# Routing two of four token batches of a mixture inside the memory attention ahead of it

## The reference, cut to what matters

```
x1: n = rmsnorm(layernorm(x)) * w;  K rows: n and the memory's keys;  attention over both
    g = sigmoid(layernorm(x) @ Wg + bg); x += the attended value mixed with layernorm(x) by g
f1: xn = layernorm(x)
    p = softmax(xn @ gate_w + gate_b)           # 8 experts
    two experts of largest p, shares p / (p_1 + p_2 + 1e-9)
    y = mlp_shared(xn) + sum over the two of share * mlp_expert(xn)   # 128 -> 512 gelu -> 128
    x = x + xn + y
```

## Time and profile before

| | |
|---|---|
| median of three runs | 2326.48 us |
| the profiled execution, its own time | 2327.09 us |
| its span, first to last instruction | 2325.2 us |
| busy in the span: PE, DVE, ACT, POOL | 76%, 57%, 47%, 32% |
| memory attention, first VectorE to last VectorE instruction | 884.0 to 990.4 us |
| first mixture, its routing and shared expert | 991.3 to 1113.1 us |
| first mixture, its 39 routed blocks, gather and add | 1113.1 to 1284.1 us |

### The profile page before, as it was taken

The page is one execution under the profiler, slowest core; times in us unless marked ns, Lnnn a source line. Parts: engine busy times, 40 slices in busy tenths (PEclk is TensorE's granted clock), DMA queues, the critical chain, the costliest instruction groups (busy, mean ns, idle before and its releaser), DMA issues. The chain is left out here.

```text
span 2325.2 us, 39403 instructions
## 1 busy us (share of the span) xinstructions
PE 1763.3 (76%) x14513; PEld 1214.8 (52%) x14513; DVE 1321.2 (57%) x3525; ACT 1103.7 (47%) x2265; POOL 746.2 (32%) x713
## 2 busy tenths in 40 slices
PE   3887561799996996859996685887788868751994
PEld 1555441545553664646896452655555535451774
DVE  2888578512235774563343465885379979851223
ACT  3676440333345776723442243773357657610431
POOL 1223200271364321057354002331223232156453
PEclk9888795699997998968998686999879969955997
DMA  4111272036624101112576001000000010011224
GB/s 154 83 82 83 90 241 69 15 104 168 181 54 171 78 2 47 28 40 99 172 234 206 10 1 33 24 20 10 3 1 2 2 37 29 11 45 66 69 77 139
DMA packets 143730, 173.19 MB, mean 74 GB/s; under 512 B 20913, under 2 KB 118897, under 8 KB 142609
## 3 DMA queue, kind: packets, MB, share of 16 engines
q1 hardware_dynamic: 123956, 129.09, 18.0%
q0 software_dynamic: 13248, 28.21, 3.6%
q10 hardware_dynamic: 6336, 13.37, 1.5%
HBM read 126.84 MB, written 79.05 MB: 89 GB/s over the span
## 5 line engine op out<-in xcount | busy, mean ns | idle before, releaser
L2773 POOL DMA_INDIRECT f_back<-f_ys,f_row x158 | 151.7, 960 | 175.8 <-DVE f_ys L2934 146.6
L2766 POOL DMA_INDIRECT f_slots<-f_pay,f_slot x128 | 124.6, 973 | 66.0 <-issue 38.1
L874 PE MATMUL a_AV<-a_vx,a_pT 128*64 128x18 f32 (+1 forms) x3072 | 115.1, 224 | 33.0 <-DVE a_two L544 15.3
L874 PEld LDWEIGHTS a_AV<-a_vx,a_pT 128*64 128x64 f32 x3072 | 105.9, 146 | 62.2 <-issue 28.6
L736 ACT ACTIVATE a_e<-a_e 128x512 f32<-128x512 f32 x192 | 110.2, 622 | 59.0 <-DVE a_e L566 58.9
L861 PE MATMUL a_TP<-ident,a_e 128*128 128x128 f32 x768 | 108.0, 285 | 19.9 <-ACT a_e L736 19.3
L741 ACT COPY a_pT<-a_TP 128x512 f32<-128x512 f32 x192 | 103.5, 588 | 39.5 <-PE a_TP L861 39.4
L861 PEld LDWEIGHTS a_TP<-ident,a_e 128*128 128x128 f32 x768 | 89.2, 146 | 57.5 <-ACT a_e L736 48.3
L566 DVE TENSOR_TENSOR a_e<-a_S,a_mx 128x1024 f32<-128x1024 f32 x96 | 117.3, 1222 | 2.9
L850 PE MATMUL a_S<-a_kbd,a_qT 64*64 64x512 f32 x768 | 114.2, 670 | 1.0 <-issue 0.6
L3000 ACT ACTIVATE f_h<-f_H,f_wt 128x256 f32<-128x256 f32 x156 | 67.1, 474 | 81.2 <-PE f_H L3096 81.2
(11 more groups left out here) (481 smaller groups left out, 4573.3 us busy)
## 6 DMA issues: line engine op xcount, KB each, us to landing
f_wt<-in_f_ew SPq DMA_DIRECT2D x39, 584.0 KB
f_slots<-in_blank SPq DMA_DIRECT2D x1, 18576.0 KB
f_wt<-in_f_leaf SPq DMA_DIRECT2D x94, 98.0 KB, 2.0
f_pay<-f_back SPq DMA_DIRECT2D x8, 1024.0 KB, 8.1
f_xs<-f_slots SPq DMA_DIRECT2D x47, 144.0 KB
memory_x_k<-w_stage ACTq DMA_DIRECT2D x24, 256.0 KB, 3.1
f_slots<-in_blank SPq DMA_DIRECT2D x1, 5760.0 KB
f_xs<-leaf_slots SPq DMA_DIRECT2D x22, 256.0 KB, 3.3
```

What stands on the lines that cost most here:

```text
L874: last = pe.matmul(AV[64 * c:64 * c + 64, 2 * hp * W1:2 * (hp + 1) * W1], pT[:, hp, 64 * c:64 * c + 64], vx[:, g % 2, t, c, 2 * hp:2 * hp ...
L2766: pool.indirect_dma_start(out=slots[:, :], out_offset=bass.IndirectOffsetOnAxis(ap=slot[:, c, t:t + 1], axis=0), in_=pay[:, c, t, :], in_o ...
L2773: pool.indirect_dma_start(out=back[:, :], out_offset=bass.IndirectOffsetOnAxis(ap=row[:, i % RR, t:t + 1], axis=0), in_=ys[:, i % RY, t, : ...
```

## The change: what it does

The routing code becomes a class `Router`, whose tiles live from memory attention to the end of the mixture. The mixture has its own function `mixture` (f3 keeps `routed`). Batch 0 (groups 0 and 1 of the attention) and batch 1 (groups 2 and 3) are routed in memory attention: for the batch that is begun in step s (s = 2 and 4), statistics and scaling stand in step s, the eight transposes in s+1, logits, softmax and choice in s+2, places and slot numbers in s+3. Batch 0's 16 indirect DMAs are issued there too, behind the last inverse root. Batch 1's are the first in the mixture. The six small loads of the router and the shared expert's weights (0.6 MB) are loaded at the start of memory attention. TensorE's order in the mixture is now shared group 0, turn and logits 2, shared 1, place 2, turn and logits 3, shared 2, place 3, shared 3 to 7. The ones, triangle and selection tiles of `place` become bfloat16.

```diff
@@ class Router (new)
+    def load(self, sp):
+        d, tag = self.d, self.tag
+        sp.dma_start(self.router[:, :], d[f"{tag}_router"]).then_inc(self.setup_in.sem, 16)
+        sp.dma_start(self.rb[:, :], d[f"{tag}_rb"]).then_inc(self.setup_in.sem, 16)
+        sp.dma_start(self.rev[:, :], d["rev"]).then_inc(self.setup_in.sem, 16)
+        sp.dma_start(self.trif[:, :], d["tri_all"]).then_inc(self.setup_in.sem, 16)
+        sp.dma_start(self.first[:, :], d["first"]).then_inc(self.late_in.sem, 16)
+        sp.dma_start(self.ids[:, :, :], d["ids"].rearrange("p (c t) -> p c t", c=2)).then_inc(self.late_in.sem, 16)
...
+    def scatter(self, pool, b):
+        k, tag = self.k, self.tag
+        if b == 0:
+            pool.wait_ge(k.slots_in[tag], k.slots_loads[tag])
+        pool.wait_ge(self.padded.sem, 1 if b < self.AHEAD else 2)
+        pool.wait_ge(self.slot_ready.sem, self.slot_ready.after(b))
+        pool.wait_ge(self.copied.sem, self.copied.after(b))
+        for c in range(2):
+            for j in range(self.BT):
+                at = self.slot[:, c, self.BT * b + j:self.BT * b + j + 1]
+                pool.indirect_dma_start(out=k.slots[tag][:, :], out_offset=bass.IndirectOffsetOnAxis(ap=at, axis=0),
+                                        in_=self.pay(b)[:, c, j, :], in_offset=None).then_inc(self.scattered.sem, 16)
...
+    def begin(self, v):
+        v.wait_ge(self.setup_in.sem, 64)
+        v.tensor_copy(self.tri[:, :], self.trif[:, :]).then_inc(self.tri_made.sem, 1)
...
+    def scale(self, v, b, j):
+        if b >= self.NBAT:
+            return
+        if j == 0:
+            v.wait_ge(self.rstd_ready.sem, self.rstd_ready.after(b))
+        t = self.BT * b + j
+        ins = v.tensor_scalar(self.pay(b)[:, 0, j, 0:P], self.k.x[:, t, :], self.mv[:, t, 0:1], self.rstd[:, t:t + 1], ALU.subtract, ALU.mult)
+        if j == self.BT - 1:
+            ins.then_inc(self.xn_ready.sem, 1)
...
+    def take_logits(self, v, b, fill):
+        lg, s, shape = self.lg, self.span(b), [P, self.BT, self.E]
+        if b:
+            v.wait_ge(self.slot_ready.sem, self.slot_ready.after(b - 1))
+        v.wait_ge(self.logits.sem, self.logits.after(b))
+        ins = v.tensor_tensor(lg[:, 0, :, :], self.LG[:, 0:self.W].rearrange("p (t e) -> p t e", e=self.E), bc(self.rb[:, :], 1, shape), ALU.add)
+        ins.then_inc(self.logits_taken.sem, 1)
+        v.wait_ge(self.logits_taken.sem, self.logits_taken.after(b))
+        self.link(v, v.tensor_reduce(self.top[:, 0, s], lg[:, 0, :, :], AX.X, ALU.max), lambda: fill(0))
+        if self.shared:
+            v.tensor_tensor(self.pe_[:, :, :], lg[:, 0, :, :], bc(self.top[:, 0, s], 2, shape), ALU.subtract).then_inc(self.gap_ready.sem, 1)
+            fill(1)
...
+    def take_turned(self, act, b, n):
+        act.wait_ge(self.x_turned.sem, self.x_turned.after(b, n + 1))
+        if b and not self.shared:
+            act.wait_ge(self.logits.sem, self.logits.after(b - 1))
+        act.copy(self.xTall[:, 2 * b + n if self.shared else n, :], self.turned(n)).then_inc(self.xT_ready.sem, 1)
+    def copy_rows(self, act, b):
+        act.wait_ge(self.xn_ready.sem, self.xn_ready.after(b))
+        act.copy(self.pay(b)[:, 1, :, 0:P], self.pay(b)[:, 0, :, 0:P]).then_inc(self.copied.sem, 1)
...
+    def place(self, pe, b):
+        E, W = self.E, self.W
+        pe.wait_ge(self.picked.sem, self.picked.after(b))
+        pe.wait_ge(self.ones_made.sem, self.ones_made.after(b))
+        pe.wait_ge(self.tri_made.sem, 1)
+        if b:
+            pe.wait_ge(self.places_taken.sem, self.places_taken.after(b - 1))
+        sb = self.sel[:, :, :].rearrange("p t e -> p (t e)")
+        pe.matmul(self.places[:, 0:W], self.tri[:, :], sb, start=True, stop=False)
+        for j in range(1, self.BT):
+            pe.matmul(self.places[:, E * j:W], self.ones[:, :], sb[:, 0:W - E * j], start=False, stop=False)
+        pe.matmul(self.places[:, 0:W], self.ones[:, :], self.before[:, b, :, :].rearrange("p t e -> p (t e)"), start=False, stop=True)\
+            .then_inc(self.placed.sem, 1)
@@ -1906,6 +2163,9 @@
     eT = ph.sb("eT", [P, GT, 2, P])
     hh = ph.sb("hh", [P, GT, P])
     PJ, TP, AV, S = ph.ps("PJ", [P, 2, 512]), ph.ps("TP", [P, 2, 512]), ph.ps("AV", [P, 2, 512]), ph.ps("S", [P, GT, 2, SL])
+    RT = ph.ps("RT", [P, 512])
+    r.banks(lambda n: RT[:, :] if n else PJ[:, 1, :], RT[:, :], RT[:, :])
+    batch = {GT * b // 2 + 2: b for b in range(r.AHEAD)}
     setup_in, cleared = ph.counter("setup_in"), ph.counter("cleared")
     ctx_in = [ph.counter(f"ctx_in{r}", 16) for r in range(4)]
     var_ready, root_ready, nmr_ready = ph.counter("var_ready"), ph.counter("root_ready"), ph.counter("nmr_ready")
@@ -1926,6 +2186,9 @@
         @block.sync
         def _(sp):
             sp.dma_start(flat(mask[:, :, :]), d["mask2"]).then_inc(setup_in.sem, 16)
+            r.load(sp)
+            WR = d["f1_sh"].shape[1]
+            sp.dma_start(k.f0w[:, NB * SL:NB * SL + WR], d["f1_sh"]).then_inc(k.shared_in, 16)
             src = d["ctx"].rearrange("(t p) d -> p t d", p=P)
             for sem in k.projected:
                 sp.wait_ge(sem, k.projections)
@@ -1947,6 +2210,11 @@
                 pool.wait_ge(var_ready.sem, var_ready.after(g))
                 pool.tensor_tensor(root[:, g % 2, :, :].rearrange("p a t -> p (a t)"), var[:, g % 2, :, :].rearrange("p a t -> p (a t)"),
                                    k.neghalf[:, 0:2 * GT], ALU.pow).then_inc(root_ready.sem, 1)
+                if g == 0:
+                    r.prepare(pool)
+                if g - 4 in (0, 2):
+                    r.root(pool, (g - 4) // 2)
+            r.scatter(pool, 0)
         @block.vector
         def _(v):
@@ -2004,20 +2272,38 @@
                 xg = k.x[:, GT * g:GT * g + GT, :]
                 v.scalar_tensor_tensor(xg, hh[:, :, :], 0.5, xg, ALU.mult, ALU.add).then_inc(x_updated.sem, 1)
+            def no_fill(j):
+                pass
             v.wait_ge(cleared.sem, 1)
+            r.begin(v)
             for i in steps:
                 if within(i):
                     shift(i)
+                if i - 3 in batch:
+                    r.give_slots(v, batch[i - 3])
                 if within(i + 2):
                     norm(i + 2)
                 if within(i - 1):
                     take_values(i - 1)
+                if i in batch:
+                    v.wait_ge(x_updated.sem, x_updated.after(i - 1))
+                    r.norm_stats(v, batch[i])
+                if i - 2 in batch:
+                    r.take_logits(v, batch[i - 2], no_fill)
                 if within(i + 2):
                     shift_mean(i + 2)
                 if within(i + 1):
                     bias_gate(i + 1)
                 if within(i + 2):
                     weigh_features(i + 2)
+                if i in batch:
+                    for j in range(r.BT):
+                        r.scale(v, batch[i], j)
+                if i - 2 in batch:
+                    r.make_shares(v, batch[i - 2], no_fill)
+                    r.pick(v, batch[i - 2], no_fill)
+                    r.weigh(v, batch[i - 2])
         @block.scalar
         def _(act):
@@ -2083,6 +2369,9 @@
             act.wait_ge(cleared.sem, 1)
             for i in steps:
+                if i - 2 in batch:
+                    r.take_turned(act, batch[i - 2], 0)
+                    r.take_turned(act, batch[i - 2], 1)
                 if within(i - 1):
                     take_weights(i - 1)
                 if within(i + 1):
@@ -2095,6 +2384,9 @@
                     normalize(i + 2)
                 if within(i + 1):
                     open_gate(i + 1)
+                if i - 2 in batch:
+                    r.gaps(act, batch[i - 2])
+                    r.copy_rows(act, batch[i - 2])
         @block.tensor
         def _(pe):
@@ -2164,15 +2456,25 @@
             for i in steps:
                 if within(i):
                     score(i)
+                if i - 3 in batch:
+                    r.place(pe, batch[i - 3])
+                if i - 2 in batch:
+                    r.make_logits(pe, batch[i - 2])
                 if within(i - 1):
                     turn_weights(i - 1)
                 if within(i + 1):
+                    if i - 2 in batch:
+                        pe.wait_ge(r.xT_ready.sem, r.xT_ready.after(batch[i - 2], 1))
                     turn(i + 1)
                 if within(i - 1):
                     weigh(i - 1)
                 if within(i + 1):
                     project(i + 1)
                     make_gate(i + 1)
+                if i - 1 in batch:
+                    b = batch[i - 1]
+                    r.turn_x(pe, b, 0, (products_taken.sem, products_taken.after(i + 1)))
+                    r.turn_x(pe, b, 1, (r.places_taken.sem, r.places_taken.after(b - 1)) if b else None)
     ph.close()
@@ def mixture (new; what is not shown is as in routed)
+        def _(pool):
+            r.pad(pool, payB[:, :])
```

(68 more changed lines are left out.)

449 lines of the change are left out of this document (added).

## The result

The changed kernel took 2337.51 us (median of seven runs, 2331.30 to 2340.05), the kernel before 2326.48 beside it: ratio 1.0037, 95% interval 1.0024 to 1.005, so slower, by 0.4%. The forecast was 2339.

The account below looks back on a forecast made before the run. The prediction took chains to bound both stretches: a ring without slack in memory attention, TensorE's order in the mixture. From 2327.1 us, +37.6 and -25.5 gave 2339.2, against the median 2338.6; it said 2339, range 2325 to 2350.

Parts of the forecast that it names:

- rival D: Added work fits the ring's idle time; memory attention grows by less than 18 us, total about 2313; chance 0.13.
- Start: Start of memory attention: VectorE waits for four set-up loads before its first instruction, +2.0 us.
- The ring: Memory attention's chain VectorE, ScalarE, TensorE has no slack; whatever is put between two of these lengthens the step in full.
- logits 0: Memory attention, batch 0: logits ahead of the weights' transposes on TensorE delay the values, +4.2 us.
- The low clock: Memory attention: TensorE's idle spells end at 1.2 GHz and slow the work behind them; 0 to 17.7 us, 10 taken.
- rival C: All four stretches of memory attention run at 1.2 GHz, adding 17.7 us; total 2346 to 2352; chance 0.15.
- the 27.6: Forecast growth of memory attention in us with TensorE at its higher clock throughout.
- Choice and places: Memory attention: TensorE's transposes and values wait behind place, which waits for VectorE's choice; +6.2 and +5.0 us.
- Place in bfloat16: TensorE's place matmuls take 0.7 us in bfloat16, against 1.7 in float32.
- Mixture: From mixture start S, first block at S+96.3 instead of S+121.8, -25.5 us; TensorE, not the writes, ends the stage.
- rival F: Batch 0's writes take over 2.7 us each and outlast memory attention; at 3.1, total 2345; chance 0.02.
- rival E: Mixture gains 20 us or less because TensorE stays at 1.2 GHz after its wait; 2344 and up; chance 0.05.

Follow-up runs that it names:

- two_mended: Changed kernel with root 3 ahead of batch 1's writes, logits and places behind the attended values, set-up wait two steps later: 2309.8 us, 0.994 of the kernel before.
- filler: Changed kernel with ten and three useless matmuls in TensorE's idle spells ahead of the two places: 2336.8 us, 1.0036 of the kernel before.
- place_behind_2: Changed kernel with only TensorE's place moved behind the attended values in memory attention, on a usual chip: 2341.4 us, 1.0067 of the kernel before.
- after_again: The changed kernel once more, unaltered, beside the second set of experiments: 2335.7 us, 1.005 of the kernel before.
- logits_behind: Changed kernel with only the logits moved behind the attended values and taken at VectorE's step end: 2332.5 us, 1.0029 of the kernel before.
- place_behind: Changed kernel with only TensorE's place moved behind the attended values, on the slower chip: 2479.1 us, 1.0079 of the kernel before.

## Why the prediction was right, and where it was not

The time, the sign and the balance of the two stretches came out as forecast (rival D's bound was a growth of 18; it was 33.7). That the median lies within 1.5 us of 2339 is in part luck: the forecast sum was +12.1, the rows of the two stretches give +6.6, and the medians +11.0. Step by step:

*Start:* +1.9 forecast as 2.0, and returned by two_mended.

*The ring.* I take the growth of the distances between takings of values (x_rs), before against after, and the forecast terms at the higher clock that fall between them:

| what lies between | measured | forecast |
|---|---|---|
| statistics 0 | +3.0 | 2.4 |
| logits 0 | +7.2 | 4.2 |
| take_logits, statistics 1, choice and place 0 | +10.3 | 9.3 |
| logits 1 | +7.2 | 4.2 |
| choice and place 1 | +5.2 | 5.0 |

Ahead of the first taking stand +1.7, and -0.9 between the first two; with these the column gives the 33.7. The steps of before are themselves uneven, 11.1 where the clock stayed up and 12.1 to 12.8 where it fell, so the single rows carry about a microsecond of that.

*The low clock.* It came behind all four spells, which was rival C's condition, but memory attention grew by 6 us over the 27.6, not by 17.7, and less than the 10 that I took. The excess lies in the logits steps, 3.0 each: moving the logits out of the ring shortened them by 11.8 where their waits alone were put at 8.4, and 8.7 of it was left at the end. The term was too large because it let each stretch run at 1.2 GHz to the end of its values. From the start of the logits to the taking of the values stand 8.8 and 9.8 us; I estimate 5.8 at the higher clock, from the forecast's 1.8 and 1.9 and the 2.06 of before's values (950.16 to 952.22). That leaves 3.1 and 4.1 where 5.3 were allowed, since the clock came back among the values, and before's step beside the second one was slow as well (12.2 against 11.1). By the Trainium skill (TensorE: Matmul & The Clock Gate, HAM oscillation) recurring waits pay for the lower clock each time; the trace agrees that it fell each time (0.50 to 0.53), while what was paid in the place steps was small, because another engine's path was as long. In the place steps the clock hardly counts (filler: 0.6 and 1.2, where 3.9 and 3.2 were allowed for), and this shows the step of the prediction that failed in its mechanism, if not in its size:

*Choice and places.* The prediction had the values wait because `turn_weights` and `turn` stand behind `place` on TensorE. The 6.2 and 5.0 are about right, but moving place away returned nothing (place_behind_2). VectorE's own program is an equally long path: choice until 976.6, the slot numbers until 980.3, the next statistics until 981.9, values at 982.42 with 0.56 of idle time. A cost read off one engine's order was held by two. Moved together with the logits, and with the slot numbers behind the gate's bias, the order returned some 13 us (15.2 in two_mended less 1.9 for the start), 4.6 more than the logits alone. two_mended is still 18.5 above before. The largest part, 7.9, is the step of choice 0, 19.1 long, in which VectorE idles for 1.6 only; the last step is 3.5 longer, behind a wait of TensorE.

*Place in bfloat16* took 0.33 us from its start to that of the transposes (976.64 to 976.97), even at the low clock, against 0.7 taken; in float32, at the higher clock, it takes 1.95 (1050.52 to 1052.47), where the prediction has 1.7.

*Mixture.* Root 3 ready: S+26.5 forecast, VectorE goes on at S+26.2. Place 2: S+37.3 both. Place 3: S+53.9 forecast, S+51.0. First block: S+96.3 and S+94.8, so the group of 13 was 3 too long and the last piece 1.4 too short. (The prediction's own low end, 10.7 for that group, adds up to -27.8 and not to its -29.) Slots in: S+85.6 and S+85.8, so the writes did not end the stage, and rival F is out; the 16 writes of batch 0 kept to 1.26 each (983.75 to 1003.87), and not to the 3.1 or so that the Trainium skill (SBUF — State Buffer, SBUF: two separate sides) gives for such a DMA beside a copy of VectorE. They say little on that figure: VectorE stood idle for 12.6 of the 20.1 us (its wait of 12.55 ahead of 1001.84). two_mended shows the cause by taking it away: 13.3 us of the stage were the wait for root 3 and the low clock behind it.

*The 6.8 us between profile and median.* Five executions with this same mixture code on the usual chips took 94.8, 94.8, 96.4, 101.1 and 101.1. They differ in how long TensorE is slow after the wait for root 3 (its second and fourth `yield_shared` take 3.84 and 3.81 us in the short ones, 5.5 and 6.8 in the long ones). Runs of 101.1 would put the change at +13, those of 94.8 at +6.6, and the medians differ by 11.0. This fits, and a mixture of 101.1 gains 20.7, which is next to rival E's bound of 20 and by its mechanism; but unprofiled runs have no rows, so it is argued and not shown. A rival stands beside it: the phases whose code did not change vary as much. In the profiled executions on the usual chips memory attention begins at 878.9 to 887.6, and from the first block to the end pass 1208.2 to 1217.2 us; after_again has the same two stretches as the first profile of the changed kernel and is 4.5 us longer.

## What to carry to other kernels

Work moved into a software pipeline should be put behind the instructions of its ring on every engine it touches, and not only on the one whose wait is seen: logits and places in front of the ring, a wait for set-up loads, and one inverse root behind 16 writes cost 25.9 us, and without them the same change is 0.6% faster than the kernel before instead of 0.4 to 0.5% slower. A wait of TensorE can cost more than its length, as the work behind it ran at half the clock: the wait of 11.3 us for root 3 cost 13.3. Before moving work ahead, ask what the receiving stage pays per batch: here the second batch cost as much as it returned, and one batch did as well as two.

## What the runs showed of the hardware that was not expected

The same instructions behind the same wait of 11 to 13 us ran 6.3 us apart from one execution to the next (94.8 and 101.1): the granted clock over the 16 us from just ahead of the work behind that wait was 0.83 in the short execution (after, 1050 to 1066) and 0.70 in a long one (logits_behind, 1043 to 1059), and over the next 26 us 1.00 against 0.74. Why it stays low longer no run shows. Ten useless matmuls held the clock at 1.00 through an 11 us spell, and bought 0.6 us there. And one chip ran the kernel before 5.6% slower (2458 us), and the edit of place_behind 5.9% slower (2479 against 2341), with idle spells of 15 to 17 us on single engines, for which its profiles name no cause.
